# Cross-attention context given features-first by the host, split straight from SBUF, and a shorter last key tile

## The chip, the core and the metric

The kernel runs on one core of a Trainium2 chip. The metric is the device time of one launch in microseconds (us); three runs of the kernel before gave 3094.23, 3101.20 and 3119.88 us. On this machine a change of about 1% is what a measurement can tell from none.

## The reference, cut to what matters

The kernel is one block with two gated attentions on 32 batches of 100 rows of 512 features. The change touches the first, a cross-attention in which 100 queries look at 722 context rows with 16 heads of 32 features:

```
q, k, v = _layernorm(x), ctx_1024, ctx_1024            # (32,100,512), (32,722,512)
qh = (q @ wq + bq) -> (b, 16, 100, 32)
kh = (k @ wk + bk) -> (b, 16, 722, 32)
vh = (v @ wv + bv) -> (b, 16, 722, 32)
scores = softmax(einsum('bhqd,bhkd->bhqk', qh, kh))
x = x + tanh(g) * (einsum('bhqk,bhkd->bhqd', scores, vh) ... @ wo + bo)
```

Everything is float32. The kernel gets that accuracy from TensorE by splitting each operand into a high part (type fp32r) and the rest (`lo = x - hi`) and adding three products: hi hi, hi lo, lo hi.

## The kernel before, in words

There are four stages, one after the other: `stage_queries` (projects the queries of all batches), `stage_cross` (the cross-attention, 32 batches), `stage_rows` and `stage_self`. The change lies in `stage_cross` and in the load that `stage_queries` starts for it. The engines run programs of their own, in a fixed order, and meet at semaphores.

For TensorE both operands of `context @ wk` must have the 512 features on the partitions, as four blocks of 128 (`KT` = 4), while the context in memory has rows of 512 features. So per batch six tiles of up to 128 rows (`CT` = 6, the last with 82 rows) are loaded (`load_rows`, L106 to L110), turned by TensorE (`turn`, four transposes for each tile, L649) into a PSUM bank, copied out by ScalarE as `ct_hi` (L519), and VectorE writes `ct_lo` = bank - `ct_hi` (L582).

The work of a batch comes in a planned order, the same for all engines (`batch_plan`, L368). It has a front: the value projections of this batch (24 parts of three to six products, L664 to L668) mixed with 16 `peak` matmuls (a maximum of the scores for each query and head, L679), with four `shift` steps: TensorE transposes four peaks (L686) and VectorE writes minus the peak into `q_stack` (L599). It ends with the last two value parts around `scores 0`. Then come 18 slots, h = 0 to 17. Slot h holds `scores h` (for h = 1 to 15: six matmuls of 100 columns, one for each key tile, L697), then a piece of the **next** batch's first work (six `turn`s and then eight `keys` products of two parts each, L658 to L662; `WORK_AFTER` says how many pieces a slot has), in slot 1 the last `shift`, and from slot 2 on `mix h-2` (six matmuls of 200 columns, L710). For each head ScalarE makes two exponentials from the scores (L537 and L541) and VectorE their difference (L608), the low part of the probabilities.

These waits matter here. `scores h` needs the exponentials of head h-2, since the score banks are two (L694). `mix 0` needs the last `shift` of the batch (L704), because the shift bank lies in the mix bank. `keys 0` needs the turned columns. A `turn` needs the copy and the subtraction of two pieces before it (L642), since the `work` banks are two. Because every engine follows the plan in order, VectorE's last `shift` (slot 1) stands behind all that slots 0 and 1 give VectorE.

SyncE issues the DMAs: at the start of each batch's round the load of the context for the batch after next (L472, L473), then the copies of the keys into `k_stack`, 12 DMAs for each of four blocks (L453), then the stores.

Of the kernel before, what the change touches and what calls it, by code (L numbers as in the profile page):

```python
# [26 lines left out]
P = 128  # L27
# [66 lines left out]
class Shared:  # L94
# [3 lines left out]
    def __init__(self, nc, ctx):  # L98
        m = Memory(nc, ctx, "e_")
        self.ident = m.sb("ident", [P, P])  # L100
        self.rows = m.sb("rows", [P, CT, D])
        self.raw_w = [m.sb(f"raw_w{n}", [P, KT, D]) for n in range(2)]
        self.ident_in, self.rows_in = m.sem("ident_in"), m.sem("rows_in")
        self.w_in = [m.sem(f"w_in{n}") for n in range(2)]

    def load_rows(self, engine, context, b):  # L106
        whole = (CT - 1) * P
        engine.dma_start(self.rows[:, 0:CT - 1, :], context[b, 0:whole, :].rearrange("(t p) d -> p t d", p=P)
                         ).then_inc(self.rows_in, 16)
        engine.dma_start(self.rows[0:C_LAST, CT - 1, :], context[b, whole:C, :]).then_inc(self.rows_in, 16)  # L110
# [14 lines left out]
def stage_queries(nc, shared, x, wq, bq, ident_dram, q_parts, context, wk, wv):  # L125
    with ExitStack() as ctx:
# [41 lines left out]
        def _(sp):  # L168
# [22 lines left out]
            shared.load_rows(sp, context, 0)  # L191
# [131 lines left out]
CPAD = CT * P  # L323
# [9 lines left out]
PR = 4  # L333
# [27 lines left out]
WORK = [("turn", t) for t in range(CT)] + [("keys", n) for n in range(2 * KT)]  # L361
# [3 lines left out]
WORK_AFTER = (1, 1, 2, 1, 1, 1, 1, 2, 1, 1, 2, 1, 1, 2, 1, 1, 1, 1)  # L365
# [17 lines left out]
A_USES = CT + CT + 2 * KT  # L383
A_FIRST = CT + 2 * KT


def work_use(kind, index, b):


    if kind == "values":  # L390
        return index, A_FIRST + b * A_USES + index
    at = WORK.index((kind, index))
    return (at, at) if b is None else (CT + at, A_FIRST + b * A_USES + CT + at)


def stage_cross(nc, shared, context, bk, neg_ident_dram, q_parts, mix_parts, prob_sums, next_weights):
    with ExitStack() as ctx:
        m = Memory(nc, ctx, "c_")
        ident, rows, raw_w = shared.ident, shared.rows, shared.raw_w
        rows_in, w_in = shared.rows_in, shared.w_in  # L400
# [7 lines left out]
        k_stack = m.sb("k_stack", [SROWS, H, CPAD], F32R)  # L408
# [13 lines left out]
        cleared = m.sem("cleared")  # L422
# [22 lines left out]
        def _(sp):  # L445
# [18 lines left out]
            sp.wait_ge(cleared, 2)  # L464
            for half in range(2):
                stack_queries(sp, 0, half)
            for n in range(KT):
                sp.wait_ge(work_lo, CT + 2 * n + 2)
# [29 lines left out]
        def _(act):  # L498
# [7 lines left out]
            def emit(kind, i, part, b, with_next=False):  # L506
                if part < PARTS.get(kind, 1) - 1:
                    return
                if kind in ("values", "turn", "keys"):
# [7 lines left out]
                    elif kind == "turn":  # L517
                        r = c_rows(i)
                        ins = act.activation(ct_hi[:, :, i * P:i * P + r],  # L519
                                             bank[:, 0:KT * r].rearrange("p (k c) -> p k c", k=KT), ACT.Copy)  # L520
# [30 lines left out]
            act.wait_ge(cleared, 6)  # L551
# [7 lines left out]
        def _(dve):  # L559
# [3 lines left out]

            split_weights(0, wk_hi, wk_lo)
            dve.wait_ge(consts_in, 32)

            def emit(kind, i, part, b, stored_before=True):
                if part < PARTS.get(kind, 1) - 1:
                    return
                if kind in ("values", "turn", "keys"):  # L570
# [8 lines left out]
                    elif kind == "turn":  # L579
                        r = c_rows(i)  # L580
                        cols = slice(i * P, i * P + r)
                        ins = dve.tensor_tensor(ct_lo[:, :, cols],  # L582
                                                bank[:, 0:KT * r].rearrange("p (k c) -> p k c", k=KT),
                                                ct_hi[:, :, cols], ALU.subtract)
# [39 lines left out]
            dve.wait_ge(cleared, 6)  # L624
# [9 lines left out]
        def _(pe):  # L634
            pe.wait_ge(consts_in, 32)

            def emit(kind, i, part, b):
                if kind in ("values", "turn", "keys"):
# [5 lines left out]
                    if kind == "turn":  # L644
                        if i == 0:
                            pe.wait_ge(rows_in, 32 if b is None else b * 32 + 64)
                        r = c_rows(i)
# [3 lines left out]
                    elif kind == "keys":  # L651
                        n, half = divmod(i, 2)
                        cols = HALVES[half]
                        if n == 0 and part == 0:

                            tile_end = -(-cols.stop // P)
                            pe.wait_ge(work_lo, work_use("turn", tile_end - 1, b)[1] + 1)
# [30 lines left out]
                elif kind == "scores":  # L688
# [6 lines left out]
                    for t in range(CT):  # L695
                        col = t % (CT // 2) * S
# [936 lines left out]
```

## Time and profile before

| | |
|---|---|
| median of three runs | 3101.2 us (3094.23 to 3119.88) |
| the profiled execution: its span, first to last instruction | 3103.1 us |
| TensorE matmul busy | 2836.2 us, 91% of the span, 18144 matmuls |
| TensorE weight loads | 2523.8 us, 81% |
| VectorE, ScalarE, GpSimd | 1932.9 us (62%), 1365.9 us (44%), 156.7 us (5%) |
| mean granted TensorE clock | 0.942 of full speed |
| DMA | 377.65 MB, mean 122 GB/s |

The profile gives no other time for its execution than the span; the span is 1.9 us above the median of the runs, so what lies around it is small against all that follows. The batches of `stage_cross` fill the time from about 137 to about 2186 us of the span. A busy share is an average over stages with different limits; the rows further down are read from the timeline of one batch. In a timeline, merged instructions have the start of the first one, and matmuls overlap in their pipeline: what a group costs TensorE is the time from its start to the start of what comes next, not its busy time.

### The profile page before, as it was taken

Reading aid. Unit: us, or ns where it says so; the run is one execution under the profiler, and the core shown is the slowest. Engines: PE = TensorE matmul, PEld = TensorE weight load, DVE = VectorE, ACT = ScalarE, POOL = GpSimd, SP = SyncE. Lnnn points to the kernel's source line nnn. Section 1 sums busy time; section 2 is a strip of 40 time slices with the busy share of each in tenths; the row PEclk is TensorE's granted clock in tenths of the full one; section 3 lists DMA queues with packets and bytes.
Section 4 is the critical chain, followed back from the end, with each engine's and each line's share of the span. In section 5 each row is a group of like instructions: output and inputs, shape, how many; then the busy total and the mean of one; then the engine's idle time right before and its main releaser. Section 6 shows DMA issues by size and latency. Waiting matters only on the chain. (4 is left out here: it accounts for less than half of the span.)

```text
span 3103.1 us, 55035 instructions
## 1 busy us (share of the span) xinstructions
PE 2836.2 (91%) x18144; PEld 2523.8 (81%) x18144; DVE 1932.9 (62%) x3059; ACT 1365.9 (44%) x3087; POOL 156.7 (5%) x154
## 2 busy tenths in 40 slices
PE   6799999999999999999999999999599994988878
PEld 5788889888998899888988899888477773777766
DVE  5556776677667766777667766776566652444434
ACT  2344455445554555445554555444333332333333
POOL 0100000000000000000000000000122220011011
PEclk9899999999999999999999999999699996778888
DMA  6445434543454344443444344443499997666653
GB/s 184 138 111 122 113 91 115 121 122 90 107 121 120 100 98 117 121 112 90 114 121 123 90 106 120 114 107 98 114 185 189 196 166 144 125 120 122 131 113 78
DMA packets 374881, 377.65 MB, mean 122 GB/s; under 512 B 128376, under 2 KB 275736, under 8 KB 374844
## 3 DMA queue, kind: packets, MB, share of 16 engines
q1 hardware_dynamic: 324252, 358.12, 50.7%
q10 hardware_dynamic: 50592, 19.06, 2.8%
q8 instruction: 20, 0.33, 0.0%
q14 instruction: 17, 0.14, 0.0%
HBM read 162.51 MB, written 72.57 MB: 76 GB/s over the span
## 5 line engine op out<-in xcount | busy, mean ns | idle before, releaser
L608 DVE TENSOR_TENSOR c_parted<-c_prob,c_parted 128x600 fp32r<-128x600 f32 x512 | 401.1, 783 | 423.5 <-ACT c_prob L541 422.4
L537 ACT ACTIVATE c_parted<-c_pair 128x600 fp32r<-128x600 f32 x512 | 343.7, 671 | 329.8 <-PE c_pair L697 325.0
L594 DVE TENSOR_REDUCE c_peak<-c_pair 100x1 f32<-100x724 f32 x512 | 450.4, 906 | 32.6 <-PE c_pair L679 21.9
L697 PE MATMUL c_pair<-c_q_stack,c_k_stack 100*128 100x100 f32 x3072 | 414.9, 272 | 0.0
L697 PEld LDWEIGHTS c_pair<-c_q_stack,c_k_stack 100*128 100x128 f32 x3072 | 394.1, 195 | 4.9
L710 PE MATMUL c_mix<-c_parted,c_v 128*66 128x200 f32 x3072 | 381.9, 261 | 2.1 <-DVE c_q_stack L599 2.0
L89 PE MATMUL c_work<-c_ct_hi,c_wk_hi 128*128 128x362 f32 (+1 forms) x1024 | 362.1, 354 | 6.2 <-DVE c_k_lo L588 5.3
L515 ACT ACTIVATE c_v<-c_work 128x512 fp32r<-128x512 f32 x192 | 115.4, 601 | 526.7 <-PE c_work L91 526.7
L710 PEld LDWEIGHTS c_mix<-c_parted,c_v 128*66 128x66 f32 x3072 | 330.6, 140 | 19.8 <-DVE c_q_stack L599 7.3
L541 ACT ACTIVATE c_prob<-c_pair 128x600 f32<-128x600 f32 x512 | 341.1, 666 | 0.0
L90 PE MATMUL c_work<-c_ct_lo,c_wk_hi 128*128 128x362 f32 (+1 forms) x1024 | 337.3, 329 | 0.0
L91 PE MATMUL c_work<-c_ct_hi,c_wk_lo 128*128 128x362 f32 (+1 forms) x1024 | 337.2, 329 | 0.0
L89 PE MATMUL c_work<-c_wv_hi,c_ct_hi 128*128 128x512 f32 (+1 forms) x768 | 313.5, 408 | 1.0 <-DVE c_k_lo L588 1.0
L90 PE MATMUL c_work<-c_wv_lo,c_ct_hi 128*128 128x512 f32 (+1 forms) x768 | 303.4, 395 | 0.0
L91 PE MATMUL c_work<-c_wv_hi,c_ct_lo 128*128 128x512 f32 (+1 forms) x768 | 302.4, 394 | 0.0
L1361 ACT ACTIVATE s_prob<-s_scores,s_shift 106x100 f32<-106x100 f32 x512 | 167.6, 385 | 272.1 <-DVE s_shift L1426 272.1
L679 PE MATMUL c_pair<-c_k_stack,c_q_stack 96*100 96x362 f32 x1024 | 259.7, 335 | 3.3
L679 PEld LDWEIGHTS c_pair<-c_k_stack,c_q_stack 96*100 96x100 f32 x1024 | 164.8, 166 | 81.5 <-DVE c_peak L594 31.5
L588 DVE SCALAR_TENSOR_TENSOR c_k_lo<-c_work,c_key_bias,c_k_hi 128x362 fp32r<-128x362 f32 (+1 forms) x256 | 151.4, 592 | 127.2 <-ACT c_k_hi L529 127.2
L529 ACT ACTIVATE c_k_hi<-c_work,c_key_bias 128x362 fp32r<-128x362 f32 (+1 forms) x256 | 143.9, 563 | 172.2 <-PE c_work L91 141.4
L89 PEld LDWEIGHTS c_work<-c_ct_hi,c_wk_hi 128*128 128x128 f32 x1024 | 196.1, 192 | 6.7 <-DVE c_k_lo L588 5.6
L90 PEld LDWEIGHTS c_work<-c_ct_lo,c_wk_hi 128*128 128x128 f32 x1024 | 195.3, 191 | 0.0
(162 smaller groups left out, 4442.8 us busy)
## 6 DMA issues: line engine op xcount, KB each, us to landing
c_k_stack<-c_k_hi SPq DMA_DIRECT2D x1024, 90.2 KB, 2.1
c_k_stack<-c_k_lo SPq DMA_DIRECT2D x512, 90.2 KB, 2.1
e_rows<-in_ctx SPq DMA_DIRECT2D x32, 1280.0 KB
s_q_stack<-qk_parts SPq DMA_DIRECT2D x48, 400.0 KB
s_k_stack<-qk_parts SPq DMA_DIRECT2D x48, 400.0 KB
c_q_stack<-q_parts ACTq DMA_DIRECT2D x186, 100.0 KB, 2.5
mix_parts<-c_mixed SPq DMA_DIRECT2D x64, 200.0 KB, 3.0
r_parts<-mix_parts SPq DMA_DIRECT2D x50, 256.0 KB, 6.9
```

The lines of the kernel that those rows point to most:

```text
L89: pe.matmul(out, left_hi, right_hi, start=first, stop=False)
L90: pe.matmul(out, left_hi, right_lo, start=False, stop=False)
L91: return pe.matmul(out, left_lo, right_hi, start=False, stop=last)
L537: act.activation(parted[i % PR][:, :, 0, :].rearrange("p (a t) s -> p a t s", a=2), logits, ACT.Exp).then_inc(exp_hi_done, 1)
L541: act.activation(prob[i % 2][:, :, :].rearrange("p (a t) s -> p a t s", a=2), logits, ACT.Exp).then_inc(exp_done, 1)
L588: ins = dve.scalar_tensor_tensor(k_lo[n % 2][:, cols], bank[:, 0:cols.stop - cols.start], key_bias[:, n:n + 1], k_hi[n % 2][:, cols], ALU. ...
L594: dve.tensor_reduce(peak[:, i:i + 1], pair[i % 2][0:S, :, 0:HALF], AX.XY, ALU.max).then_inc(peak_done, 1)
L608: dve.tensor_tensor(p[:, :, 1, :], prob[i % 2][:], p[:, :, 0, :], ALU.subtract).then_inc(p_lo_done, 1)
L679: last = pe.matmul(pair[i % 2][0:S, bank, 0:HALF], q_stack[0:STACK, i, :], k_stack[0:STACK, i, cols], start=True, stop=True)
L697: last = pe.matmul(pair[i % 2][:, t // (CT // 2), col:col + S], k_stack[:, i, t * P:(t + 1) * P], q_stack[:, i, :], start=True, stop=True)
L710: last = pe.matmul(mix[g % 2][0:VW, at * 2 * S:(at + 1) * 2 * S], v[:, t, i, :], parted[i % PR][:, t, :, :].rearrange("p a s -> p (a s)"), ...
L1361: last = act.activation(prob[:, j, k, :], scores[0:QR, j, k * S:(k + 1) * S], ACT.Exp, bias=shift[:, at:at + 1], scale=-1.0, accum_out=tot ...
```

## The change

The host hands over the context as (32, 512, 722). The load brings it as four blocks of 128 features by 722 rows into `columns`. The transposes, their PSUM banks and their `work` semaphores are gone: in slot 0 ScalarE copies blocks 0 and 1 of `columns` to `ct_hi` and VectorE subtracts, in slot 1 blocks 2 and 3, with two semaphores of their own (`ct_hi_done`, `ct_lo_done`). The 16 parts of the key products stand one in each slot from slot 2. The score matmul of the last key tile loads 82 weight columns and writes 82 partitions, where before it loaded 128 with 46 zero columns, and the mix matmul of that tile reads 82 partitions; `k_stack` has rows of 722 and not of 768.

```
-        self.rows = m.sb("rows", [P, CT, D])
+        self.columns = m.sb("columns", [P, KT, C])
...
+    def load_columns(self, engine, context, b):
+        engine.dma_start(self.columns[:], context[b].rearrange("(k p) c -> p k c", p=P)).then_inc(self.columns_in, 16)
...
-WORK = [("turn", t) for t in range(CT)] + [("keys", n) for n in range(2 * KT)]
+WORK = [("split", k) for k in range(KT)] + [("keys", n) for n in range(2 * KT)]
...
-WORK_AFTER = (1, 1, 2, 1, 1, 1, 1, 2, 1, 1, 2, 1, 1, 2, 1, 1, 1, 1)
+WORK_AFTER = (2, 2) + (1,) * H
...
-        k_stack = m.sb("k_stack", [SROWS, H, CPAD], F32R)
+        k_stack = m.sb("k_stack", [SROWS, H, C], F32R)
...   SyncE
-            sp.wait_ge(cleared, 2)
+            sp.wait_ge(cleared, 1)
...
-                sp.wait_ge(work_full, b * A_USES + WORK.index(("turn", CT - 1)) + 1)
-                shared.load_rows(sp, context, b + 1)
+                sp.wait_ge(ct_lo_done, b * KT + KT)
+                shared.load_columns(sp, context, b + 1)
...   GpSimd
-            fills = [(k_stack[:, :, C:CPAD], 0.0), (k_stack[STACK:SROWS, :, 0:C], 1.0),
-                     (v[:, CT - 1, :, :], 0.0), (v[0:C_LAST, CT - 1, :, 2 * HD:2 * HD + 1], 1.0),
-                     (v[:, 0:CT - 1, :, 2 * HD + 1:VW], 0.0), (v[:, 0:CT - 1, :, 2 * HD:2 * HD + 1], 1.0)]
+            fills = [(k_stack[STACK:SROWS, :, :], 1.0), (v[:, :, :, 2 * HD + 1:VW], 0.0),
+                     (v[:, :, :, 2 * HD:2 * HD + 1], 1.0)]
...   ScalarE
+                if kind == "split":
+                    after = 0 if b is None else b + 1
+                    act.wait_ge(columns_in, after * 16 + 16)
+                    if i == 0 and b is not None:
+                        act.wait_ge(work_full, work_use("values", CT - 1, b)[1] + 1)
+                    act.activation(ct_hi[:, i, :], columns[:, i, :], ACT.Copy).then_inc(ct_hi_done, 1)
...   VectorE
+            for i in range(2):
+                dve.memset(pair[i][P // 2:P, 1, (CT // 2 - 1) * S:CT // 2 * S], 0.0).then_inc(padded, 1)
...
+                if kind == "split":
+                    after = 0 if b is None else b + 1
+                    dve.wait_ge(ct_hi_done, after * KT + i + 1)
+                    dve.tensor_tensor(ct_lo[:, i, :], columns[:, i, :], ct_hi[:, i, :], ALU.subtract
+                                      ).then_inc(ct_lo_done, 1)
...   TensorE
-                        for k in range(KT):
-                            last = pe.transpose(bank[:, k * r:(k + 1) * r], rows[0:r, i, k * P:(k + 1) * P],
-                                                ident[0:r, 0:r])
...
+                        if i == 0:
+                            after = 0 if b is None else b + 1
+                            pe.wait_ge(ct_lo_done, after * KT + (part + 1) * KT // K_PARTS)
...
-                        last = pe.matmul(pair[i % 2][:, t // (CT // 2), col:col + S],
-                                         k_stack[:, i, t * P:(t + 1) * P], q_stack[:, i, :],
+                        col, r = t % (CT // 2) * S, c_rows(t)
+                        last = pe.matmul(pair[i % 2][0:r, t // (CT // 2), col:col + S],
+                                         k_stack[:, i, t * P:t * P + r], q_stack[:, i, :],
...
-                        last = pe.matmul(mix[g % 2][0:VW, at * 2 * S:(at + 1) * 2 * S], v[:, t, i, :],
-                                         parted[i % PR][:, t, :, :].rearrange("p a s -> p (a s)"),
+                        r = c_rows(t)
+                        last = pe.matmul(mix[g % 2][0:VW, at * 2 * S:(at + 1) * 2 * S], v[0:r, t, i, :],
+                                         parted[i % PR][0:r, t, :, :].rearrange("p a s -> p (a s)"),
...   host
+    arrays["ctx_1024"] = np.ascontiguousarray(arrays["ctx_1024"].transpose(0, 2, 1))
```

## Rows read from the trace of the kernel before

**Rows 1.** The page, first part: busy time of each engine, share, instructions.
```profile
PE 2836.2 (91%) x18144; PEld 2523.8 (81%) x18144; DVE 1932.9 (62%) x3059; ACT 1365.9 (44%) x3087; POOL 156.7 (5%) x154
```

**Rows 2.** Timeline of TensorE: start, us, engine, line, out<-in, shape, count.
```profile
1015.00 0.77 PE L697 MATMUL c_pair<-c_q_stack,c_k_stack 100*128 100x100 f32 x6
...
1017.02 0.60 PE L649 MATMUL c_work<-e_ident,e_rows 128*128 128x128 f32 x4
...
1027.23 0.72 PE L710 MATMUL c_mix<-c_parted,c_v 128*66 128x200 f32 x6
1027.79 0.79 PE L697 MATMUL c_pair<-c_q_stack,c_k_stack 100*128 100x100 f32 x6
1028.41 0.39 PE L89 MATMUL c_work<-c_ct_hi,c_wk_hi 128*128 128x362 f32 x1
...
1029.47 0.72 PE L710 MATMUL c_mix<-c_parted,c_v 128*66 128x200 f32 x6
...
1050.94 0.79 PE L697 MATMUL c_pair<-c_q_stack,c_k_stack 100*128 100x100 f32 x6
```

**Rows 3.** Timeline of ScalarE in the same batch, with the idle time before.
```profile
1017.22 0.60 ACT L515 ACTIVATE c_v<-c_work 82x512 fp32r<-82x512 f32 x1 [0.18 <-PE c_work L91]
1017.72 0.58 ACT L519 ACTIVATE c_ct_hi<-c_work 128x512 fp32r<-128x512 f32 x1
1018.27 0.67 ACT L537 ACTIVATE c_parted<-c_pair 128x600 fp32r<-128x600 f32 x1
...
1019.38 0.61 ACT L519 ACTIVATE c_ct_hi<-c_work 128x512 fp32r<-128x512 f32 x1
```

**Rows 4.** Timeline of VectorE in the same batch.
```profile
1017.85 0.69 DVE L576 TENSOR_TENSOR c_v<-c_work,c_v 82x512 fp32r<-82x512 f32 x1
...
1019.53 0.78 DVE L608 TENSOR_TENSOR c_parted<-c_prob,c_parted 128x600 fp32r<-128x600 f32 x1 [0.39 <-ACT c_prob L541]
1020.23 0.68 DVE L582 TENSOR_TENSOR c_ct_lo<-c_work,c_ct_hi 128x512 fp32r<-128x512 f32 x1
1020.95 0.57 DVE L599 TENSOR_TENSOR c_q_stack<-c_mix,c_neg_ident 4x400 fp32r<-4x400 f32 x1
```

**Rows 5.** ScalarE by line and shape: a copy whose source is SBUF.
```profile
L501 ACT ACTIVATE c_wv_hi<-e_raw_w 128x2048 fp32r<-128x2048 f32 x1 | 1.9, 1912 | 0.0
```

**Rows 6.** TensorE's weight loads by shape, 250 to 2100 us: count, busy us, mean ns.
```profile
L697 PEld LDWEIGHTS c_pair<-c_q_stack,c_k_stack 100*128 100x128 f32 x2820 | 354.7, 192 | 4.5
...
L89 PEld LDWEIGHTS c_work<-c_wv_hi,c_ct_hi 128*82 128x82 f32 x120 | 18.1, 151 | 4.9
```

**Rows 7.** Table of stretches: length, busy time of each engine, clock, DMA share, GB/s.
```profile
1004.20:1013.70 9.50, 9.46 (x47) 7.55 (x46) 9.04 (x13) 1.42 (x3) 0.00 (x0) 1.00 0.60 175
1013.70:1017.00 3.30, 3.30 (x19) 2.38 (x18) 1.92 (x3) 1.57 (x3) 0.00 (x0) 1.00 0.00 0
```

**Rows 8.** The same view around two falls of TensorE's clock and one rise.
```profile
1458.60:1462.00 3.40, 2.51 (x23) 2.12 (x21) 2.98 (x6) 3.38 (x7) 0.00 (x0) 1.00 0.00 0
1462.00:1465.50 3.50, 3.50 (x19) 3.50 (x20) 2.50 (x4) 1.57 (x4) 0.00 (x0) 0.51 0.00 0
1465.50:1470.00 4.50, 4.50 (x43) 4.47 (x43) 3.16 (x6) 4.22 (x8) 0.00 (x0) 1.00 0.00 0
2155.00:2158.40 3.40, 1.55 (x16) 1.55 (x17) 2.13 (x3) 1.62 (x4) 0.00 (x0) 1.00 0.02 5
2158.40:2186.00 27.60, 27.60 (x152) 27.60 (x151) 12.29 (x18) 15.91 (x26) 0.00 (x0) 0.50 0.00 1
148.00:151.20 3.20, 3.20 (x12) 3.20 (x11) 2.29 (x1) 0.88 (x1) 1.39 (x4) 0.50 0.60 154
151.40:154.60 3.20, 3.20 (x21) 3.20 (x20) 1.11 (x2) 1.13 (x2) 0.00 (x0) 1.00 0.10 26
```

**Rows 9.** Timeline of TensorE: first mix of the last batch.
```profile
2156.85 0.77 PE L710 MATMUL c_mix<-c_parted,c_v 128*66 128x200 f32 x6 [2.02 <-DVE c_q_stack L599]
```

**Rows 10.** Timeline, start of the stage: the first key product.
```profile
147.51 0.64 PE L89 MATMUL c_work<-c_ct_hi,c_wk_hi 128*128 128x362 f32 x1 [0.92 <-DVE c_ct_lo L582]
```

More of the change, by code:

```diff
@@ L100, in __init__ @@
         self.ident = m.sb("ident", [P, P])
-        self.rows = m.sb("rows", [P, CT, D])
+        self.columns = m.sb("columns", [P, KT, C])
         self.raw_w = [m.sb(f"raw_w{n}", [P, KT, D]) for n in range(2)]
-        self.ident_in, self.rows_in = m.sem("ident_in"), m.sem("rows_in")
+        self.ident_in, self.columns_in = m.sem("ident_in"), m.sem("columns_in")
         self.w_in = [m.sem(f"w_in{n}") for n in range(2)]
[L106 to L110, printed above, removed]
+    def load_columns(self, engine, context, b):
+        engine.dma_start(self.columns[:], context[b].rearrange("(k p) c -> p k c", p=P)).then_inc(self.columns_in, 16)
     def load_weights(self, engine, weights):
@@ L190, in _ @@
             load(1)
-            shared.load_rows(sp, context, 0)
+            shared.load_columns(sp, context, 0)
             load(2)
@@ L322 @@
 CT = -(-C // P)
-CPAD = CT * P
 C_LAST = C - (CT - 1) * P
@@ L380, in batch_plan @@
     return plan
-A_USES = CT + CT + 2 * KT
-A_FIRST = CT + 2 * KT
+A_USES = CT + 2 * KT
+A_FIRST = 2 * KT
 def work_use(kind, index, b):
@@ L391, in work_use @@
         return index, A_FIRST + b * A_USES + index
-    at = WORK.index((kind, index))
-    return (at, at) if b is None else (CT + at, A_FIRST + b * A_USES + CT + at)
+    return (index, index) if b is None else (CT + index, A_FIRST + b * A_USES + CT + index)
 def stage_cross(nc, shared, context, bk, neg_ident_dram, q_parts, mix_parts, prob_sums, next_weights):
@@ L398, in stage_cross @@
         m = Memory(nc, ctx, "c_")
-        ident, rows, raw_w = shared.ident, shared.rows, shared.raw_w
-        rows_in, w_in = shared.rows_in, shared.w_in
+        ident, columns, raw_w = shared.ident, shared.columns, shared.raw_w
+        columns_in, w_in = shared.columns_in, shared.w_in
         neg_ident = m.sb("neg_ident", [HPT, HPT])
@@ L508, in emit @@
                     return
-                if kind in ("values", "turn", "keys"):
+                if kind == "split":
[4 more added lines that the diff above has]
+                    act.activation(ct_hi[:, i, :], columns[:, i, :], ACT.Copy).then_inc(ct_hi_done, 1)
+                elif kind in ("values", "keys"):
                     local, use = work_use(kind, i, b)
@@ L516, in emit @@
                                              bank[0:r, :].rearrange("p (h d) -> p h d", d=HD), ACT.Copy)
[L517 to L520, printed above, removed]
                     else:
@@ L550, in _ @@
                 emit(kind, i, part, None)
-            act.wait_ge(cleared, 6)
+            act.wait_ge(cleared, 3)
             with act.Fori(0, B - 1) as b:
@@ L569, in emit @@
                     return
-                if kind in ("values", "turn", "keys"):
+                if kind == "split":
[3 more added lines that the diff above has]
+                                      ).then_inc(ct_lo_done, 1)
+                elif kind in ("values", "keys"):
                     local, use = work_use(kind, i, b)
@@ L578, in emit @@
                                                 v[0:r, i, :, 0:HD], ALU.subtract)
[L579 to L584, printed above, removed]
                     else:
@@ L637, in emit @@
             def emit(kind, i, part, b):
-                if kind in ("values", "turn", "keys"):
+                if kind in ("values", "keys"):
                     local, use = work_use(kind, i, b)
@@ L643, in emit @@
                         pe.wait_ge(work_hi, use - 1)
[L644 to L647, printed above, removed]
-                        for k in range(KT):
-                            last = pe.transpose(bank[:, k * r:(k + 1) * r], rows[0:r, i, k * P:(k + 1) * P],
-                                                ident[0:r, 0:r])
-                    elif kind == "keys":
+                    if kind == "keys":
                         n, half = divmod(i, 2)
                         cols = HALVES[half]
-                        if n == 0 and part == 0:
-                            tile_end = -(-cols.stop // P)
-                            pe.wait_ge(work_lo, work_use("turn", tile_end - 1, b)[1] + 1)
+                        if i == 0:
+                            after = 0 if b is None else b + 1
+                            pe.wait_ge(ct_lo_done, after * KT + (part + 1) * KT // K_PARTS)
                         for k in range(part * KT // K_PARTS, (part + 1) * KT // K_PARTS):
@@ L719, in _ @@
             pe.wait_ge(w_lo_done, 2)
-            pe.wait_ge(cleared, 6)
+            pe.wait_ge(cleared, 3)
+            pe.wait_ge(padded, 2)
             with pe.Fori(0, B - 1) as b:
```

8 lines of the change are left out of this document (4 added, 4 removed).

## Prediction

> **What bounds the kernel now.** I read the page first: TensorE is busy for 91% of the span, VectorE for 62%, ScalarE for 44% [rows 1]. The chain of waits covers only the end of the program, in the last stage, so it says nothing of the stage that changes. The timeline of one batch, around 1015 us, is the view that decides. In a late slot TensorE has no gap: mix from 1027.23, scores from 1027.79, a key part from 1028.41, the next mix at 1029.47 [rows 2], that is 0.56 + 0.62 + 1.06 = 2.24 us, against two exponentials on ScalarE, 1.11 us from the start of the pair to the next instruction [rows 3], and one subtraction of 0.78 us on VectorE [rows 4]. So there TensorE is the bound, and work taken from it is time. In slots 0 to 3 it is otherwise: ScalarE's instructions stand one behind another from 1017.22 on [rows 3]. That is where the change puts all its copies.
>
> I count time from the start of scores 0, T = 1015.00 [rows 2]. The first turn stands at T+2.02, and scores 15 start at 1050.94, T+35.94 [rows 2].
>
> **Transposes removed.** 24 a batch. I don't sum them: as slots 0 to 3 are bound elsewhere, their price is no gain by itself; I lay the new order out instead and compare where scores 15 start.
>
> **Copies added.** ScalarE: 722 columns from SBUF. 512 columns take 0.60 us and 2048 from SBUF 1.91 us [rows 3, 5], 0.85 ns a column, so 0.78 us; the next one starts 0.03 to 0.10 earlier than the end, so one each 0.70. VectorE: 512 columns 0.69, 600 columns 0.78 [rows 4], so 722 take 0.91, one each 0.84. Bounds: 0.75 to 0.85 and 0.85 to 0.95; the shapes are near, so I take the middle.
>
> ScalarE after the change: the value copy at T+2.22 as now, split 0 at 2.72, split 1 at 3.42, exponentials of head 1 from 4.12, split 2 at 4.12 + 1.11 = 5.23, split 3 at 5.93, ending 6.71 [rows 3]. VectorE: value subtraction at 2.85 as now, split 0 at 3.53, split 1 at 4.37 to 5.28; the subtraction of head 1 starts 1.26 after its exponentials (1018.27 to 1019.53) [rows 3, 4], so 5.38; split 2 at 6.08, split 3 at 6.92, then the last shift 7.76 to 8.33 (0.57) [rows 4].
>
> TensorE: scores 1 at 2.02, scores 2, both over by 3.3. The first key part needs two subtracted blocks: 5.28 plus 0.05, so 5.33, ending 6.39. **Mix 0 needs the last shift, which stands behind four splits on VectorE: 8.38.** So TensorE stands still for 2.0 us and, after 1.06 us of work, for 2.0 us again. Behind mix 0 wait scores 3 and everything else; the pairs of score banks don't let it run ahead. From 8.38 there is no further wait: scores 3 at 8.94, and the exponentials of head 2 ended long before.
>
> **The shorter tile.** In the score group each matmul follows its weight load. A load of 128 columns takes 192 ns, one of 82 takes 151 [rows 6]: 41 ns for each head, with 100 moving columns at under 50 ns too short to hide the longer load. A slot is then 2.20. Bounds 0 and 41 ns; the row is of the same type, so 41. The key loads with that shape are the nearest check on a rule of the Trainium skill, TensorE: Matmul & The Clock Gate, Weight-path perf modes: a fast load is used for 128 weights of a type that isn't FP32, so 82 columns would lose it. The trace disagrees, 151 against 192 ns; by the rule the sum would be about 20 us higher.
>
> Scores 15 thus start at 8.94 + 12 x 2.20 = 35.34, before 35.94, and scores 15 save 0.04 more: **0.64 us a batch, 31 times, 20 us**. The last batch has no splits and saves 16 x 0.04 = 0.6 us.
>
> **TensorE's clock.** The sum above holds at full clock. The last batch of the trace shows what a wait at this place does. It has no turns; mix 0 waited 2.02 us for the same shift [rows 9]; in those 3.4 us TensorE was busy for 1.55, and then the granted clock was 0.50, the lower of its two levels (1.2 against 2.4 GHz), for 27.60 us, though scores and mixes followed without a gap [rows 8]. In a batch with turns the clock fell too after a stretch with 2.51 of 3.40 us busy, and was 0.51 for 3.50 us and 1.00 after [rows 8]. The new order has about 1.06 us of work in the 5.1 us before mix 0, less than either. I expect the clock to fall in nearly every batch. Up to mix 0 that is free: a key part of six matmuls at half clock (12 starts in 3.20 us [rows 8], some 1.8 us) ends before 8.38. From there each microsecond at half costs half of it. How long? Between 3.5 us, partly in the gap (1.2 us or so lost), and 27.6 us (13.8 lost) [rows 8]. Key products did bring the clock back after a half-clock stretch without a gap (148.00 to 151.20, then 1.00) [rows 8], and each new slot has a key part, so the short end is nearer. I take two stretches of the kind, from 8.38 to 14.0: 2.8 us lost a batch. Net per batch 2.8 - 0.64 = 2.16 us more; 31 times 67 us.
>
> **The rest.** The load is one DMA of 1.48 MB instead of two of 1.44 together. The old one went at 175 GB/s and was over by 1013.70 [rows 7]; the new is needed at T+2.72, 4 us later, and even at 115 GB/s it fits in the 13.5 us from 1004.2. SyncE's new wait is long fulfilled when it comes (the subtractions were a batch before), so nothing is queued behind it. Its 48 key copies start when keys 1 is done, about 3 us earlier, at their own pace; rows of 722 may start off a boundary, for which I take 0, up to a doubling, as `ct_hi` has such rows already in the 151 ns load [rows 6]. Fewer GpSimd fills: 0, hidden behind the first key products. Two VectorE memsets at the start, under 0.5 us each, are before its wait for ScalarE's first weight copy: 0. At the start the first key product stands at 147.51 [rows 10] behind six turns, each with its copy and subtraction; now two splits of 0.84 on VectorE stand there instead of six subtractions of 0.5 to 0.7, and no transposes: I estimate 4 us saved (0 to 6).
>
> **Sum.** 3103.1 - 4 - 0.6 + 67 = 3165 us. That is against the profiled execution's span; the median of the runs is 1.9 lower, which I leave out.
>
> **Rivals.**
> A. The clock falls but comes back as it did at 1465.50, so some 1.2 us a batch: 3103.1 - 4.6 + 31 x 0.56 = 3116. For it: the fall with turns in the trace. Against: the last batch. It becomes a loss of over 1% from 1.75 us a batch.
> B. The clock stays full, and only the schedule counts: 3103.1 - 4.6 - 20 = 3079. For it: 2.0 us gaps are short, and the batch at 1015 with its own gaps kept the clock (its key part takes 1.06 us, the pace of full clock) [rows 2]. Against: the last batch [rows 9]. The Trainium skill, TensorE: Matmul & The Clock Gate, Part 4: PE-mode transpose, says that transposes don't count as busy for the gate as matmuls do; then the old slots 0 to 3 would look as idle as the new ones, and removing the turns would not change the clock. By that rule B is the outcome. But the batch at 1015 kept its clock through gaps and turns, where the last batch, with a gap and no turns, lost it, so the trace speaks against the rule.
> C. The two gaps don't come, since the splits are faster or slip beside other work; then scores 3 start at about T+4.9 and each batch gains 4.0 + 0.64 us: 3103.1 - 4.6 - 144 = 2954. Against: [rows 3, 4], which leave ScalarE and VectorE no room for it. Halfway, one gap at full clock saved, is 3103.1 - 4.6 - 31 x 2.6 = 3018.
> D. The 82-column load saves nothing while the clock falls: 3185. Or the load of the columns comes late: each us of it is 31 us.
>
> **Chances.** Forecast, with D: 0.62 for a loss of 1.75 to 6.5 us a batch, 3133 to 3280 by itself. A 0.11, B 0.15, C and what lies between B and C 0.12. Within 1% means 3070 to 3132: A and B. A little of A may lie above, so slower 0.63, same 0.25, faster 0.12. Range: 3075 (B with a little room) to 3235 (5 us a batch); beyond lie C and the long half-clock cases, about 2 in 10.
>
> **What would show it.** In the timeline of a middle batch: four copies of 0.78 us and four subtractions of 0.91; the first key part at T+5.3 and mix 0 at T+8.4, released by the shift (c_q_stack L599 before); a weight load of about 151 ns in the sixth place of each score group; in the table of stretches a granted clock near 0.5 in a part of every batch after T+5, where it was 1.00. The prediction is wrong if mix 0 starts before T+7, if the clock stays at 1.00 in most batches, or if it stays half for 20 us in each.

## The result, and the profile after

The changed kernel takes 3152.0 us (median of 4 runs, 3146.5 to 3155.2), the one before 3097.7 us on the same chip (4 runs, 3092.0 to 3119.9). The ratio is 1.016, 95% interval 1.012 to 1.021: slower, though the kernel issues 768 matmuls fewer and moves no more data. The profiled execution of after took 3149.1 us, with a span of 3146.8, 43.7 us more than before's.

The page of after, part 1 and the clock row of part 2 (before: [rows 1]):

```profile
PE 2818.5 (90%) x17376; PEld 2508.1 (80%) x17376; DVE 1929.1 (61%) x2997; ACT 1352.4 (43%) x3023; POOL 155.2 (5%) x151
...
PEclk9888999999999999999999999999699997677778
```

These two parts of the page give no hint: TensorE is 90% busy in place of 91%, and the clock row has the same nines over the batches, as its tenths round a clock that is low for a tenth of the time away. Two other figures do give one: the mean granted clock of the whole span is 0.901 in place of 0.942, and part 5 of the page has TensorE idle for 72.6 us before L89 (waiting for `ct_lo`) and 63.9 us before the mix (waiting for `q_stack`), 2.0 us for the mix in before. The stretch from 300 to 2000 us, which holds only batches of the changed loop, shows the clock of the loop by itself. First the row of after, then that of before; columns are TensorE, its weight loads, VectorE, ScalarE, GpSimd, granted clock, DMA share, GB/s:

```profile
300.00:2000.00 1700.00, 1595.01 (x10396) 1445.49 (x10395) 1153.63 (x1624) 816.38 (x1337) 0.00 (x0) 0.95 0.45 108
```

```profile
300.00:2000.00 1700.00, 1672.54 (x11316) 1511.70 (x11315) 1192.19 (x1725) 852.25 (x1430) 0.00 (x0) 1.00 0.45 110
```

The timeline of TensorE in one batch of after; scores 0 start at T = 1045.56 ([rows 2] has the same batch position of before):

```profile
1045.56 0.73 PE L687 MATMUL c_pair<-c_q_stack,c_k_stack 100*128 100x100 f32 x6
...
1048.14 0.81 PE L687 MATMUL c_pair<-c_q_stack,c_k_stack 100*128 100x100 f32 x6
1050.85 0.43 PE L89 MATMUL c_work<-c_ct_hi,c_wk_hi 128*128 128x362 f32 x1 [1.90 <-DVE c_ct_lo L572]
...
1054.14 1.24 PE L701 MATMUL c_mix<-c_parted,c_v 128*66 128x200 f32 x6 [2.02 <-DVE c_q_stack L597]
1055.17 1.32 PE L687 MATMUL c_pair<-c_q_stack,c_k_stack 100*128 100x100 f32 x6
...
1059.13 0.75 PE L687 MATMUL c_pair<-c_q_stack,c_k_stack 100*128 100x100 f32 x6
...
1061.33 0.75 PE L687 MATMUL c_pair<-c_q_stack,c_k_stack 100*128 100x100 f32 x6
```

Two waits of 1.90 and 2.02 us stand around one key part. Mix 0 and the scores behind it then take 1.24 and 1.32 us where the late slots take 0.72 and 0.75: the lower clock. Scores 4 start at T+13.57, and from there a slot is 2.20 us. VectorE in the same batch shows why TensorE waits: it has no idle time (before: [rows 4]).

```profile
1049.07 1.73 DVE L572 TENSOR_TENSOR c_ct_lo<-e_columns,c_ct_hi 128x722 fp32r<-128x722 f32 x2
1050.87 0.78 DVE L606 TENSOR_TENSOR c_parted<-c_prob,c_parted 128x600 fp32r<-128x600 f32 x1
1051.57 1.73 DVE L572 TENSOR_TENSOR c_ct_lo<-e_columns,c_ct_hi 128x722 fp32r<-128x722 f32 x2
1053.33 0.57 DVE L597 TENSOR_TENSOR c_q_stack<-c_mix,c_neg_ident 4x400 fp32r<-4x400 f32 x1
```

Three stretches of the batch, after (the columns as above; before: [rows 8]):

```profile
1049.00:1052.10 3.10, 1.25 (x6) 0.96 (x6) 3.02 (x5) 3.10 (x6) 0.00 (x0) 1.00 0.00 0
1052.20:1059.00 6.80, 4.86 (x23) 4.82 (x24) 3.23 (x5) 2.82 (x6) 0.00 (x0) 0.50 0.00 0
1059.00:1110.20 51.20, 51.09 (x344) 46.34 (x343) 35.50 (x52) 22.64 (x38) 0.00 (x0) 1.00 0.57 136
```

After 3.10 us with 1.25 us of work the granted clock is the lower of the two levels (1.2 GHz) for 6.8 us, then full. The trace has 29 such falls between 200 and 2150 us, 28 of 6.8 us and an early one of 20.5; with one of 13.7 us from 198.8 and one more of 6.8 from 2154.7 that is one in each of the 31 batches that have splits, from 330 us on always starting between T+6.6 and T+6.9. Before has two in that range, of 3.4 us each. A batch takes 64.85 us, before 63.00.

**Where the 43.7 us are.** Scores 0 of the first batch start at 193.5 (before 196.0): -2.5. Scores 0 of the last start 31 batches later, with a mean period of 65.14 against 63.08 in before's profile: 31 x 2.07 = +64. The last batch is 0.7 shorter. The stage so ends at 2249.1 instead of 2188.1 us, +61. The stages behind it, whose code is the same, took 897.7 us instead of 915.0: -17.3. In the thirteen traces of this case what lies behind the last mix of `stage_cross` varied from 883 to 915 us, with its code unchanged, and before's is the longest. I do not explain those 17 us.

### The profile page after: what moved, and what is told of

The parts are those of the page before. It is cut to its first block and busy times, and to the rows that moved or that the text cites. A ratio compares the mean times of both kernels' runs of the same rounds, so it can differ in the third digit from the quotient of the medians.

```text
span 3146.8 us, 52744 instructions
## 1 busy us (share of the span) xinstructions
PE 2818.5 (90%) x17376; PEld 2508.1 (80%) x17376; DVE 1929.1 (61%) x2997; ACT 1352.4 (43%) x3023; POOL 155.2 (5%) x151
## 5 line engine op out<-in xcount | busy, mean ns | idle before, releaser
L701 PE MATMUL c_mix<-c_parted,c_v 128*66 128x200 f32 (+1 forms) x3072 | 406.1, 273 | 64.0 <-DVE c_q_stack L597 63.9
L89 PE MATMUL c_work<-c_ct_hi,c_wk_hi 128*128 128x362 f32 (+1 forms) x1024 | 384.0, 375 | 76.4 <-DVE c_ct_lo L572 72.6
L701 PEld LDWEIGHTS c_mix<-c_parted,c_v 128*66 128x66 f32 (+1 forms) x3072 | 360.6, 151 | 87.5 <-issue 70.6
L687 PE MATMUL c_pair<-c_q_stack,c_k_stack 100*128 100x100 f32 (+1 forms) x3072 | 407.9, 274 | 0.0
L687 PEld LDWEIGHTS c_pair<-c_q_stack,c_k_stack 100*128 100x128 f32 (+1 forms) x3072 | 397.6, 199 | 8.1
L91 PE MATMUL c_work<-c_ct_hi,c_wk_lo 128*128 128x362 f32 (+1 forms) x1024 | 350.2, 342 | 0.0
L90 PE MATMUL c_work<-c_ct_lo,c_wk_hi 128*128 128x362 f32 (+1 forms) x1024 | 349.8, 342 | 0.0
L89 PE MATMUL c_work<-c_wv_hi,c_ct_hi 128*128 128x512 f32 (+1 forms) x768 | 314.4, 409 | 3.1 <-DVE c_k_lo L586 3.1
L89 PEld LDWEIGHTS c_work<-c_ct_hi,c_wk_hi 128*128 128x128 f32 x1024 | 206.7, 202 | 81.0 <-DVE c_ct_lo L572 62.8
L90 PEld LDWEIGHTS c_work<-c_ct_lo,c_wk_hi 128*128 128x128 f32 x1024 | 206.2, 201 | 0.0
L91 PEld LDWEIGHTS c_work<-c_ct_hi,c_wk_lo 128*128 128x128 f32 x1024 | 204.5, 200 | 0.0
```

The costliest lines, as they stand in the source:

```text
L89: pe.matmul(out, left_hi, right_hi, start=first, stop=False)
L90: pe.matmul(out, left_hi, right_lo, start=False, stop=False)
L91: return pe.matmul(out, left_lo, right_hi, start=False, stop=last)
L687: last = pe.matmul(pair[i % 2][0:r, t // (CT // 2), col:col + S], k_stack[:, i, t * P:t * P + r], q_stack[:, i, :], start=True, stop=True)
```

## The experiments

Times are medians; "before" is the kernel before on the same chip in the same comparison (3094 to 3107 us), and the ratio is against it. A **filler** is a matmul on data that is there, into a bank that the next work overwrites; its result is used by nothing. All kernels with fillers, `fill_both` first, add this to the changed kernel (`fill_turns` with another body). The experiments ran on two chips, so two kernels are best compared through their ratios to before, or by the batch period of their traces:

```
+            def fill(bank, times):
+                for _ in range(times):
+                    pe.matmul(bank[:], wk_hi[:, 0, 0:P], wk_hi[:, 0, :], start=True, stop=True)
```

### fill_both: the same schedule, with both waits filled

```
+                        if i == 0 and part == 0 and not (b is None or isinstance(b, int)):
+                            fill(work[0], 7)
...
                     if i == 0:
-                        pe.wait_ge(shift_done, b * KT + KT)
                         pe.wait_ge(work_lo, work_use("values", CT - 1, b)[1] + 1)
+                        if not isinstance(b, int):
+                            fill(work[1], 7)
+                        pe.wait_ge(shift_done, b * KT + KT)
```

The first call stands before the first key part, the second before mix 0 and ahead of the wait for the last shift.

> The changed kernel with 7 useless matmuls of 512 columns (1.6 us) put on TensorE into each of the two gaps, before the first key part and before mix 0; they write banks that nobody reads, and no wait is taken away. Clock theory: the granted clock stays at 1.00 through the middle batches, mix 0 still starts at about T+8.4, a batch takes 62.4 us and not 64.85, and the time is about 3152 - 31 x 2.4 = 3077 us. Rival, that the waits themselves cost the time: work in the gaps changes nothing, 3150 us or more.

Measured: 3067.3 us, ratio 0.992 (0.989 to 0.996). TensorE's timeline, with scores 0 at 1002.83:

```profile
1006.06 1.84 PE L637 MATMUL c_work<-c_wk_hi 128*128 128x512 f32 x7
1008.12 0.43 PE L89 MATMUL c_work<-c_ct_hi,c_wk_hi 128*128 128x362 f32 x1 [0.22 <-DVE c_ct_lo L572]
...
1009.23 1.75 PE L637 MATMUL c_work<-c_wk_hi 128*128 128x512 f32 x7
1011.23 0.78 PE L709 MATMUL c_mix<-c_parted,c_v 128*66 128x200 f32 x6 [0.25 <-DVE c_q_stack L597]
```

```profile
300.00:2000.00 1700.00, 1684.90 (x11131) 1504.06 (x11130) 1199.40 (x1690) 840.18 (x1380) 0.00 (x0) 1.00 0.46 112
```

The first key part starts at T+5.29, to 0.01 us where it did in the changed kernel, and mix 0 at T+8.40 (T+8.58 there). VectorE's order and the waits are as they were, only TensorE has something useless to do in them. The clock is 1.00, a batch takes 62.49 us. So the schedule alone would have made the kernel a little faster, as rival B has it; what made it slower is the clock: 64.85 - 62.49 = 2.36 us a batch. Times the 31 batches, with the longer first ones (65.14 in the mean), that is 82 us, and the medians are 3152.0 - 3067.3 = 85 apart (81 by the two ratios to before).

### fill_first and fill_second: one wait filled

`fill_first` has only the first of the two calls, `fill_second` only the second.

> The changed kernel with the 7 useless matmuls in the first gap only, before the first key part. Clock theory: the one gap of 2.0 us that is left before mix 0 has dense work before it, so the clock stays up in most batches: about 3080 us, at most 3110. If the gap right before mix 0 is by itself what lets the clock fall: about 3150.

> The changed kernel with the 7 useless matmuls in the second gap only, before mix 0. Clock theory: the first gap stands behind two thin score groups, so the clock still falls in a part of the batches, but the half-clock time then lies more in the waits: 3085 to 3130 us. If only the gap before mix 0 counts: 3077.

Measured: `fill_first` 3117.8 us, ratio 1.007 (1.003 to 1.011), which is a miss: I had said 3110 at most, as the one gap left would have dense work before it. It has 23 falls between 200 and 2150 us, most of 3.4 us, 95 us in all at half clock; a batch takes 64.05 us in the mean, between 62.6 and 65.8 after the first. `fill_second` 3121.3 us, ratio 1.005 (1.001 to 1.009), as forecast (3085 to 3130), has 28 falls, 180 us at half clock. Neither wait alone is the cause; either one is enough for a fall in most batches. `fill_second` shows the same loop in two patterns. Scores 0 of its first batches start at 191.42, 253.90, 317.51, 379.99, 443.59, 506.07, so 62.48 and 63.60 us apart in turn, with a fall of 3.4 us in every second batch. After some six batches it has 6.8 us at half in each, 64.85 us apart, to the end.

### fill_turns: the waits filled with transposes

As `fill_both`, but each call issues 15 transposes of the identity instead of 7 matmuls:

```
-                    pe.matmul(bank[:], wk_hi[:, 0, 0:P], wk_hi[:, 0, :], start=True, stop=True)
+                    pe.transpose(bank[:, 0:P], ident[:], ident[:])
```

> The changed kernel with 15 useless transposes of the 128x128 identity (about 1.6 us) in each gap instead of matmuls. If transposes hold the clock as the turns of the kernel before seem to have done: about 3080 us, clock 1.00 in the middle batches. If transposes don't count as work for the clock, as a page says: unchanged, about 3150 us.

Measured: 3061.6 us, ratio 0.989 (0.985 to 0.994), a batch 62.48 us. First the timeline, then the long stretch:

```profile
1007.36 1.84 PE L637 MATMUL c_work<-e_ident 128*128 128x128 f32 x15
...
1010.53 1.80 PE L637 MATMUL c_work<-e_ident 128*128 128x128 f32 x15
```

```profile
300.00:2000.00 1700.00, 1685.35 (x11563) 1525.75 (x11563) 1199.67 (x1691) 840.88 (x1380) 0.00 (x0) 1.00 0.46 112
```

1.8 us of transposes in each gap hold the clock as 1.8 us of matmuls do. This decides what the prediction had to leave between a row and a rule: the Trainium skill, TensorE: Matmul & The Clock Gate, Part 4: PE-mode transpose, has transposes not count as busy in the same way, and here these transposes of float32 data, which the trace lists as MATMUL, hold a clock that is up. Whether transposes alone would raise a low clock no run here shows. It also fits what the removed turns had been doing beside their own work, that they kept TensorE from standing still where it waits for VectorE: in before, TensorE is busy for 4.88 of the 5.80 us from 1018.20 to 1024.00, with waits of 0.37 and 0.53 us before turns. That part is argued; no run took the turns' own share away from the old order.

### tile_only and full_tile_fill: each half of the change by itself

`tile_only` is the kernel before, turns included, with the short last tile (its diff, against the kernel before, is below); `full_tile_fill` is `fill_both` with the last tile's load at 128 columns again.

```
-                        last = pe.matmul(pair[i % 2][:, t // (CT // 2), col:col + S],
-                                         k_stack[:, i, t * P:(t + 1) * P], q_stack[:, i, :],
+                        last = pe.matmul(pair[i % 2][0:r, t // (CT // 2), col:col + S],
+                                         k_stack[:, i, t * P:t * P + r], q_stack[:, i, :],
```

> The kernel before with the second half of the change alone: 82 weight columns in the last score tile, rows of 722 in k_stack, 82 partitions in the last mix matmul; transposes stay. Theory: 512 loads are 41 ns shorter and each is on TensorE's path, 21 us less than before, ratio 0.993, and the 12 key copies of a block keep their pace. Rival, that a load of 82 columns or rows off a boundary cost something: ratio 1.00 or more.

> The first half of the change alone at full clock: context by features, splits from SBUF, the last score tile with all 128 columns as before, and the 7 useless matmuls in both gaps. Theory: the order's own worth is almost nothing, since the two waits take back what the transposes cost: 20 us above the same kernel with the short tile (3067), so 3087, a batch of 63.1 us. Rival, that the splits alone are a clear gain at full clock: 3070 or less.

Measured: `tile_only` 3071.9 us, ratio 0.992 (0.989 to 0.995), a batch 62.47 us against 63.00 in before: 0.53 us, 33 ns a head. `full_tile_fill` 3081.9 us, ratio 0.994 (0.991 to 0.996), a batch 62.95 us, 0.46 more than `fill_both`. TensorE's weight loads in `tile_only`, 250 to 2100 us (before: [rows 6]):

```profile
L698 PEld LDWEIGHTS c_pair<-c_q_stack,c_k_stack 100*128 100x128 f32 x2387 | 306.7, 192 | 4.4
L698 PEld LDWEIGHTS c_pair<-c_q_stack,c_k_stack 100*82 100x82 f32 x477 | 73.0, 153 | 0.0
```

The shorter tile is a gain of its own, and nearly all that the change has at full clock: without it the new splits give 63.00 - 62.95 = 0.05 us a batch, and with it, `fill_both` against `tile_only`, -0.02 us. Removing 24 transposes a batch is worth next to nothing, as they stood where TensorE had to wait anyway. The medians alone, 0.8% apart, would hardly show the tile's gain; the periods do, as they repeat to 0.02 us within `tile_only`.

### shift_first: one wait less, and slower still

The last shift (the small subtraction for which mix 0 waits) is put ahead of the splits on VectorE. This takes the wait before mix 0 away.

```
+        if h == 0:
+            plan.append(("shift", KT - 1, 0))
         if with_next:
...
-        if h == 1:
-            plan.append(("shift", KT - 1, 0))
```

> The changed kernel with the last shift ahead of the splits, in slot 0, nothing else. By the order: mix 0 at about T+6.9 instead of 8.4, scores 4 at about T+9.9 instead of 11.1 at full clock; but the first key part waits longer, 2.5 us in one gap, so the clock still falls in most batches. 3070 to 3100 us. Rival, that the two gaps and not their sum let the clock fall: no falls, 3040.

Measured: 3204.4 us, ratio 1.032 (1.027 to 1.037). That is a miss, and on the other side: 3070 to 3100 was said. The wait before mix 0 is gone as planned. TensorE's timeline, then two stretches that together are a batch:

```profile
1018.23 0.67 PE L89 MATMUL c_work<-c_ct_hi,c_wk_hi 128*128 128x362 f32 x1 [2.46 <-DVE c_ct_lo L572]
...
1020.20 1.20 PE L701 MATMUL c_mix<-c_parted,c_v 128*66 128x200 f32 x6
1021.20 1.32 PE L687 MATMUL c_pair<-c_q_stack,c_k_stack 100*128 100x100 f32 x6
```

```profile
1016.90:1034.10 17.20, 15.87 (x71) 15.59 (x71) 8.61 (x13) 8.01 (x14) 0.00 (x0) 0.50 0.00 0
1034.10:1085.20 51.10, 49.82 (x328) 44.37 (x327) 35.41 (x51) 23.30 (x39) 0.00 (x0) 1.00 0.55 136
```

The clock is at half from 1016.90, that is already in the gap, and stays there for 17.2 us with TensorE 15.87 us busy; in the changed kernel it came back after 6.8. A batch takes 68.27 us. I had counted on fewer gaps meaning less time at half. How long the clock stays down does not follow from the sum of the gaps. Four key parts start while it is down.

### shift_first_fill: is the miss the clock alone?

As `shift_first`, with nine fillers in the one gap that is left.

```
+                        if i == 0 and part == 0 and not (b is None or isinstance(b, int)):
+                            fill(work[0], 9)
```

> shift_first (3204 us, the miss) with 9 useless matmuls of 512 columns in its one gap before the first key part. If the miss was the clock alone (17.1 us at half in each batch): no falls, a batch of about 61.2 us as worked out from the order, 3067 - 40 = 3027 us. If the order itself is worse than worked out: 3067 or more.

Measured: 3014.4 us, ratio 0.970 (0.964 to 0.977), no fall in any of the batches, a batch 61.18 us; mix 0 starts at T+7.01, where 6.9 was worked out. So the order of `shift_first` is 1.3 us a batch better than `fill_both`'s, and its loss was the clock: 68.27 - 61.18 = 7.09 us a batch, 220 us in all by the traces, 190 by the medians (3204.4 - 3014.4), whose runs of `shift_first` lie from 3193 to 3233.

The result lies 13 us below the 3027 that was said. 31 x 1.31 = 41 us from 3067 was the whole sum; it left the last batch out. There the moved shift shortens the wait before mix 0 from 2.02 us [rows 9] to 0.69, and the last batch takes 22.6 us where before and the changed kernel take 36.8 and 36.2, 14 us less. The section on `spread_fill_last` shows its lines.

### spread_fill and spread: no long wait, with and without fillers

The splits are dealt one to a slot over slots 0 to 3, with the key parts from slot 3 on, and the last shift goes first, as above. `spread_fill` adds three fillers before mix 0 and four before the first key part.

```
-WORK_AFTER = (2, 2) + (1,) * H
+WORK_AFTER = (1, 1, 1, 2, 0, 1, 1, 1, 1, 1, 1, 1, 1, 2, 1, 2, 1, 1)
```

> A version meant to beat both: last shift in slot 0, one split in each of slots 0 to 3, the first key part in slot 3, the second in slot 5, the others after, two slots doubled; with 3 useless matmuls before mix 0 and 4 before the first key part, to hold the clock. By the order, at full clock: mix 0 at T+4.2, first key part at T+6.6, second at T+9.9, a batch of about 60.5 us, so about 3067 - 2.0 x 31 = 3005 us. If the clock falls all the same: 3040 to 3080.

> The spread order (last shift in slot 0, one split in each of slots 0 to 3, key parts from slot 3) without the 7 useless matmuls. It has waits of about 1.0 and 1.2 us before mix 0 and before the first key part at full clock. If these are too short and too far apart for a fall: about the same as with the fillers, 2981 us. Clock theory, by the little work that lies between them (one mix and one score group): the clock falls in most batches, 30 to 150 us more, 3010 to 3130.

Measured: `spread_fill` 2981.4 us, ratio 0.962 (0.958 to 0.967): the fastest, 3.8% under the kernel before and some 170 us under the changed one. The batch is as worked out (60.50 us); of the 24 us below the 3005 that was said, 14 are the last batch again. `spread` 3125.4 us, ratio 1.009 (1.005 to 1.013). First `spread_fill`'s timeline and its long stretch (scores 0 at 976.98; the next batch's at 1037.48, 60.50 later), then three stretches of a batch of `spread`:

```profile
980.28 0.92 PE L637 MATMUL c_work<-c_wk_hi 128*128 128x512 f32 x3
981.32 0.75 PE L710 MATMUL c_mix<-c_parted,c_v 128*66 128x200 f32 x6
...
982.49 1.16 PE L637 MATMUL c_work<-c_wk_hi 128*128 128x512 f32 x4
983.59 0.44 PE L89 MATMUL c_work<-c_ct_hi,c_wk_hi 128*128 128x362 f32 x1
```

```profile
300.00:2000.00 1700.00, 1693.37 (x11313) 1515.02 (x11312) 1234.83 (x1745) 868.21 (x1429) 0.00 (x0) 1.00 0.47 115
```

```profile
1024.50:1030.20 5.70, 4.57 (x36) 3.78 (x35) 4.21 (x7) 4.97 (x9) 0.00 (x0) 1.00 0.00 0
1030.30:1040.50 10.20, 9.61 (x45) 9.47 (x45) 6.29 (x9) 5.91 (x10) 0.00 (x0) 0.50 0.00 0
1040.50:1090.00 49.50, 49.38 (x324) 44.53 (x324) 33.88 (x49) 20.28 (x34) 0.00 (x0) 1.00 0.59 140
```

Mix 0 now starts at T+4.34, in place of T+8.58. `spread` has the same order, and two waits that look harmless in its timeline:

```profile
1028.62 0.74 PE L701 MATMUL c_mix<-c_parted,c_v 128*66 128x200 f32 x6 [0.87 <-DVE c_q_stack L597]
...
1030.89 0.67 PE L89 MATMUL c_work<-c_ct_hi,c_wk_hi 128*128 128x362 f32 x1 [0.94 <-DVE c_ct_lo L572]
```

With them the clock falls in every batch: for 3.4 us in each of the first three, which took 61.7 to 62.0 us, and for 10.2 us in the 28 others, whose period went to 64.85 us, the very period of the changed kernel, though the time at half is 10.2 us here and 6.8 there.

### spread_fill_last: fillers in the last batch too

The expectation below takes it that the last batch loses its clock in every kernel; I had read the 27.3 us at half from 2090.3 in `spread_fill` that way, which was wrong, as the trace below shows. In this run three fillers stand before mix 0 of that batch as well:

```
-                        if not isinstance(b, int):
-                            pe.wait_ge(work_lo, work_use("values", CT - 2, b)[1] + 1)
-                            fill(work[0], 3)
+                        pe.wait_ge(work_lo, work_use("values", CT - 2, b)[1] + 1)
+                        fill(work[0], 3)
```

> spread_fill with the 3 useless matmuls before mix 0 in the last batch as well, which has no next batch and lost its clock in every kernel so far. If they hold the clock there: up to 14 us less than spread_fill, 2967 to 2975. If the rest of that batch, scores and mixes alone, lets it fall anyway: 2981.

Measured: 2998.7 us, ratio 0.968 (0.961 to 0.974), hardly to be told from `spread_fill` (0.958 to 0.967 there). There was nothing to win. The trace of `spread_fill`, without those fillers, has scores 0 of the last batch at 2065.98 and its last mix at 2087.84. First its mix 0, then the stretch of the batch, then the stretch of the fall:

```profile
2070.13 0.78 PE L710 MATMUL c_mix<-c_parted,c_v 128*66 128x200 f32 x6 [0.69 <-DVE c_q_stack L597]
```

```profile
2066.00:2088.60 22.60, 21.08 (x200) 19.80 (x198) 17.19 (x26) 19.62 (x33) 0.00 (x0) 1.00 0.00 1
2090.30:2117.60 27.30, 2.84 (x7) 2.29 (x8) 14.10 (x11) 7.84 (x7) 4.47 (x4) 0.50 0.65 193
```

The last batch ran at full clock. The fall lies behind it, at the start of `stage_rows`, where TensorE stands idle for 26.14 us. In `spread_fill_last` the last batch takes 22.62 us too, with mix 0 at T+4.15 in both, and the fall starts at 2093.8, again behind the batch (its last mix ends at 2091.4). The premise was wrong: the moved shift had already shortened the wait before mix 0 of the last batch from 2.02 to 0.69 us, and its clock stayed up. The same holds for `shift_first`, `shift_first_fill` and `spread`, whose last batches take 22.6 us. In the kernels with the shift in slot 1 the last batch takes 36.2 to 37.6 us, some 30 of them at half clock.

## Why the prediction was right

**The schedule.** Each point of the laid-out order came within 0.2 us. Splits took 0.80 and 0.91 us (0.78 and 0.91 said); the first key part stands at T+5.29 (5.33); mix 0 at T+8.58 (8.38), released by the shift of L597 as said; a late slot is 2.20 us (2.20). What made this work was laying the order out engine by engine from the rows, and not adding up the transposes' durations.

**The schedule's gain at full clock.** Said 0.64 us a batch; `fill_both` has 63.00 - 62.49 = 0.51. The term that was mis-sized is the shorter tile: 41 ns a head said, from the weight loads' difference; 33 measured in the period of `tile_only`. The load itself is 39 ns shorter (192 and 153), and some of that does not reach the path. The rest, the new order by itself, was 0.12 us of the sum (13 x 0.04 of the 0.64 are the tile's) and measured 0.05 and -0.02: nothing, or nearly.

**The clock.** The step that decides, that two waits of 2 us around a microsecond of work cost the clock in nearly every batch, was right; `fill_both` removes nothing but the idleness and gets the time back, so it is shown. Its size was somewhat too large: 2.8 us lost a batch said, 2.36 measured. The clock is at half for 6.8 us from T+6.6, and came back at T+13.4 (T+14.0 said). Past the start of mix 0 that is 4.9 us at half, and half of it is the 2.4 us lost; 5.6 us were said. Net that is 64.85 - 63.00 = 1.85 us a batch in place of 2.16, and with the longer first batches 2.07 in the mean.

The length at half was hit in part by luck. The prediction chose the short end of 3.5 to 27.6 us because each new slot has a key part. But the number of key parts that started before the clock came back was one in the changed kernel, two in `spread` and four in `shift_first` (17.1 us). So key parts did not set the length; what did stays open. The 27.60 us of [rows 8] are also not the whole of that fall: the stretch was cut at the end of the stage, and the clock of before stays at half for 61.4 us, from 2158.4 to 2219.8.

**The start.** 4 us said, 2.5 measured in scores 0. The first key product came at 143.29 (before 147.51 [rows 10]):

```profile
143.29 0.64 PE L89 MATMUL c_work<-c_ct_hi,c_wk_hi 128*128 128x362 f32 x1 [13.74 <-DVE c_ct_lo L572]
```

so 4.2 us earlier, and 1.7 of them were lost again on the way to scores 0. I did not follow where; in `fill_both`, whose start has the same code, scores 0 came at 190.5, so the start itself varies by 3 us.

**The terms put at nothing.** They held. Nothing waited for the load of the columns (7.1 us from issue to landing in the median), and a key copy took 2.2 us to land in place of 2.1. The text had the load's size wrong: 1444 KB in one DMA against 1280 and 164 KB in two is the same amount (1.48 MB), and it is for the next batch (b + 1, L473), not for the one after it. A key part at half clock would take 1.6 us by the row cited (12 starts in 3.20 us), not 1.8; neither changes the sum.

**The sum.** Said 3165 against a span of 3103.1, so +62; the stage came out at +61. That the two agree to 1 us is luck, as errors cancel: the lower loss a batch in the steady state (1.85 and not 2.16) takes off 10 us and the two falls in before, which the prediction did not count, 2; the first batches, of 67.5 and 70.9 us, which it did not have, add 9, and the start 1.5. The measured difference is smaller, +44 in the profiles and +54 in the medians, because later stages were 17 us shorter in the profile.

**The rivals.** B (full clock, 3079) is what `fill_both` shows the schedule to be worth: 3067. Its rule about transposes fell to `fill_turns`. A (a loss of 1.2 us a batch at the clock) fell by the size: 2.36. C failed on the place named for it, VectorE's queue of four splits. `shift_first_fill`, at 3014, lies near C's halfway case (3018), but not by its sum: it gains 1.82 us a batch over before, not 2.6, and the rest is the last batch and other stages. `spread_fill`, at 2981, gains 2.50 us a batch of C's 4.64. Both are other orders than the changed kernel's, and hold their clock by fillers. D's claim that the 82-column load saves nothing fell to `tile_only`. The prediction had set a rule against that row, that of the Trainium skill, TensorE: Matmul & The Clock Gate, Weight-path perf modes, by which a load of 128 weights of a type that isn't FP32 is a fast one; no run here shows a load of 128 columns to be the faster one. The trace lists these operands, fp32r in the kernel, as f32, so this case does not show whether the rule is meant for them.

## What to carry to other kernels

Before removing work from an engine that waits for another, ask what the work was filling. Where TensorE is near full use, idle time of one or two microseconds costs more than itself when it recurs in a loop: read the mean granted clock of the span, then that of a stretch of many iterations, and, if it is below 1.00, put a filler in the gap as a test. One such run separates "the schedule is worse" from "the clock fell", and here the order that looked worst (`shift_first`, 3204 us) was among the best with its gap filled (3014 us).

Look where a fall lies before giving it a cause: a fall at the end of a stage can belong to the next one. A batch at the end of a loop can also gain or lose by itself what 31 batches don't show, here 14 us.

A change that joins two edits should be timed in halves: the shorter tile gained 0.8% alone (0.53 us a batch), and was hidden under the loss of the other half.

## What the runs showed of the hardware

- **Useless matmuls made kernels faster**: 14 a batch turned 3152 us into 3067, seven turned 3125 into 2981, nine turned 3204 into 3014.
- **Transposes hold the clock as matmuls do**: 30 a batch, 3061.6 us, granted clock 1.00.
- **The time at half clock locks to the loop, in most kernels.** After the first batches it was the same in each batch of a kernel, to 0.1 us, but between kernels 6.8, 10.2 or 17.1 us, for gaps of 1.9 to 2.5 us (6.8 and 17.1) and even of 0.9 us (10.2). `fill_first` is the exception: most falls of 3.4 us, some of 6.8 or 10.2, and none in eight of 31 batches. One loop changed from one pattern to another after six batches (`fill_second`). All these lengths are whole multiples of the shortest, and the two periods of loops with a fall in each batch, 64.85 and 68.27 us, are 3.4 us apart. Two orders of work, the changed kernel and `spread`, fell into the same period of 64.85 us, though at full clock they would take 62.49 and 60.50. What decides the pattern stays open.
- The Trainium skill, TensorE: Matmul & The Clock Gate, HAM oscillation, tells of a clock that falls in each iteration of a loop because of a wait for a transfer. The same happens here with a wait for VectorE, and with two waits of 0.9 us a batch (`spread`). A single wait of 0.69 us, in the last batches, left the clock up.
